# A second attention run in double slots: the scores of two head pairs back to back, with the other steps packed between them

## The reference, cut to what matters

```python
xn = _layernorm(x, ln_gamma, ln_beta)
q = (xn @ w_q).reshape(B, SQ, NUM_HEADS, DIM_HEAD)        # 16 batches, 256 x 16 x 64
k, v = jnp.split(context @ w_kv, 2, axis=-1)
scores = jnp.einsum('bqhd,bkhd->bhqk', q * SCALE, k)
attn = jax.nn.softmax(scores, axis=-1)
out = jnp.einsum('bhqk,bkhd->bqhd', attn, v).reshape(B, SQ, INNER)
out = out @ w_out + b_out
return out * jnp.tanh(gate[0])                            # added to x
```

## Time and profile before

| what | value |
|---|---|
| median of three runs | 1820.49 us (1820.12 to 1822.55) |
| the profiled execution, its span | 1823.8 us |
| PE busy | 1709.7 us, 94% |
| DVE, ACT, POOL busy | 1313.3, 1144.5, 825.5 us (72%, 63%, 45%) |
| second attention, first to last scores | 1039.5 to 1621.8 us |
| scores of pair 16 to scores of pair 126 | 1116.9 to 1618.2 us |

### The profile page before, as it was taken

One profiled execution on the slowest core, in us unless ns is written; L12 is line 12 of the kernel. 1 busy time (PEld: TensorE's weight loads), 2 busy tenths in 40 slices (PEclk: granted clock), 3 DMA queues, 4 the chain that ended last, 5 costly groups with the idle time before them and its releaser, 6 DMA issues.

```text
span 1823.8 us, 41775 instructions
## 1 busy us (share of the span) xinstructions
PE 1709.7 (94%) x16112; PEld 1461.9 (80%) x16112; DVE 1313.3 (72%) x2808; ACT 1144.5 (63%) x2880; POOL 825.5 (45%) x1300
## 2 busy tenths in 40 slices
PE   5799999999999999999999889999999999997778
PEld 4567676679899999999999767888888888876655
DVE  4789989551707888888888486777777777668447
ACT  1377677523347777777777477777777777764330
POOL 2235433110103333333331487888888887764200
PEclk7799999999999999999999999999999999999789
DMA  7755556246876666666676722222222222111378
GB/s 187 207 134 121 128 132 120 80 155 237 295 257 211 243 244 243 243 243 243 244 241 221 243 76 65 93 65 70 63 95 66 69 63 89 53 56 48 99 209 296
DMA packets 131815, 284.99 MB, mean 156 GB/s; under 512 B 13921, under 2 KB 74593, under 8 KB 118945
## 3 DMA queue, kind: packets, MB, share of 16 engines
q1 hardware_dynamic: 110880, 169.81, 30.9%
q0 software_dynamic: 20736, 112.51, 18.1%
HBM read 199.95 MB, written 82.05 MB: 155 GB/s over the span
## 4 chain that ended last, share of the span: by engine, by line
PE 75%; DVE 10%; DMA 5%; POOL 5%; issue 4%; ACT 0%; SPq 0%; DVEq 0%; POOLq 0%; ACTq 0%
PE ps L1250 12%; PE ps L1236 12%; PE ps L1998 5%; PE ps L373 5%; PE ps L219 5%; PE ps L2029 4%; PE ps L1984 4%; PE ps L2018 4%; PE ps L379 4%; PE ps L464 3%; PE ps L440 3%; DVE NM L592 2%; POOL P L209 2%; PE ps L540 2%; PE ps L452 2%
## 5 line engine op out<-in xcount | busy, mean ns | idle before, releaser
L196 ACT ACTIVATE P<-ps,NM 128x256 f32<-128x256 f32 x512 | 236.3, 481 | 127.5 <-DVE NM L185 127.5
L209 POOL TENSOR_TENSOR P<-P,RS 128x1024 f32<-128x1024 f32 x128 | 242.9, 1903 | 73.9 <-DVE RS L203 73.5
L1236 PE MATMUL ps<-XRP,W1P 128*128 128x256 f32 x1872 | 227.1, 281 | 3.3 <-DVE W1P L1319 3.3
L1236 PEld LDWEIGHTS ps<-XRP,W1P 128*128 128x128 f32 x1872 | 220.4, 190 | 3.6 <-DVE W1P L1319 3.6
L1250 PE MATMUL ps<-W2P,HP 128*128 128x256 f32 x1872 | 221.9, 277 | 0.0
L1250 PEld LDWEIGHTS ps<-W2P,HP 128*128 128x128 f32 x1872 | 218.5, 188 | 0.0
L592 DVE TENSOR_REDUCE NM<-ps 128x2 f32<-128x512 f32 x256 | 164.4, 684 | 38.2 <-PE ps L440 36.5
L690 ACT ACTIVATE PT<-ps 128x512 f32<-128x512 f32 x256 | 139.2, 597 | 69.7 <-PE ps L452 67.5
L185 DVE TENSOR_REDUCE NM<-ps 128x2 f32<-128x512 f32 x256 | 164.6, 685 | 5.8 <-PE ps L1984 4.2
L1170 POOL DMA_INDIRECT WE<-in_we,WIX x39 | 44.3, 1135 | 269.2 <-DVE W1P L1319 208.8
L1279 ACT ACTIVATE HF<-ps,WE 128x256 f32<-128x256 f32 x312 | 129.0, 465 | 43.3 <-PE ps L1236 43.3
(11 more groups left out here) (236 smaller groups left out, 3740.2 us busy)
## 6 DMA issues: line engine op xcount, KB each, us to landing
KS<-k_scratch SPq DMA_DIRECT2D x64, 256.0 KB, 2.9
V<-v_scratch SPq DMA_DIRECT2D x16, 1024.0 KB, 6.1
k_scratch<-KVM SPq DMA_DIRECT2D x52, 256.0 KB, 3.9
QS<-q_scratch SPq DMA_DIRECT2D x96, 128.0 KB, 4.4
v_scratch<-KVM SPq DMA_DIRECT2D x40, 256.0 KB, 3.0
ys_scratch<-YS SPq DMA_DIRECT2D x39, 256.0 KB, 8.0
ctx_scratch<-CHL SPq DMA_DIRECT2D x32, 256.0 KB, 2.7
CHR<-ctx_scratch SPq DMA_DIRECT2D x16, 512.0 KB, 4.8
```

The source lines that it names most:

```text
L196: i = e.activation(self.P[u % 4][:, c, :], PS[SB[n % 3]][:, y * 256:y * 256 + 256], ACT.Exp, bias=self.NM[:, u % 4, c:c + 1], accum_out=se ...
L209: e.tensor_tensor(p, p, self.RS[:, u % 4, :].unsqueeze(2).to_broadcast([128, 4, 256]), ALU.mult).then_inc(self.s_pn, 1)
L1236: m = e.matmul(PS[p][:, hh * 256:hh * 256 + 256], W1P[i % 2][wi][:, cc * 1024 + hc * 128:cc * 1024 + hc * 128 + 128], XRP[i % 2][xi][:, cc ...
```

## The change

The same instructions are put in another order, and the banks are dealt out anew. The loop now runs over 64 double slots (`SLOTS1`) and 21 more (`TAIL1`) for the last layer. In double slot i:

- PE: scores of pairs 2i and 2i+1; one half of a result (`results_in`); turn of 2i-2; one part of queries, of index i+2 (`queries_in`); in the first two of a batch's four slots the turn of the next input; turn of 2i-1; values of 2i-3 and 2i-2; from slot 65 the steps of the last layer.
- DVE: split of 2i-5, max of 2i, split of 2i-4, max of 2i+1, result add, reciprocal of 2i, the batch's work, reciprocal of 2i+1, low half of the queries.
- ACT: exp 2i, copies of turn 2i-2, exp 2i+1, copies of turn 2i-1, high half of the queries, keys, norms.
- POOL: norms of 2i and 2i+1, keys, input, newton, fetches.

Banks: 0 to 3 scores, 4 and 5 turns, 6 (`WB`) queries and results together, 7 (`OB1`) values of even pairs in one half, values of odd pairs and the turned input in the other. Since queries and results share a bank, queries wait for the result add of their own slot, and a result waits for the low half of the queries of the slot before. A result is no longer accumulated over eight pairs: each half goes into the bank alone and is added to x by itself, so there are 64 additions instead of 32. Both splits of a slot wait for the values of both pairs (`done`).

Cut to its core:

```diff
     SB, TB, OB = (0, 1, 2), (3, 4), 5
+    SB1, TB1, OB1, WB = (0, 1, 2, 3), (4, 5), PS[7], PS[6]
...
-    QB, RB = PS[7], PS[6]
+    def results_in(i):
+        if i < 5:
+            return ()
+        if i <= SLOTS1:
+            return (i - 5,)
+        return {SLOTS1 + 1: (60, 61), SLOTS1 + 2: (62, 63)}.get(i, ())
+    def queries_in(i):
+        return tuple(d for d in ((1, 2) if i == 0 else (i + 2,)) if d < SLOTS1)
+    def values_in(i):
+        return tuple(u for u in (2 * i - 3, 2 * i - 2) if 0 <= u < U)
+    def results_before(i):
+        return sum(len(results_in(x)) for x in range(i))
...
-            w.wait_ge(a1.s_ex, 2 * u - 1)
+            w.wait_ge(a1.s_ex, 2 * (u - 1))
...
-        def queries(b, n):
+        def queries(d, added):
+            b, n = d // 4, d % 4
             w.wait_ge(s_wl, 2)
             w.wait_ge(s_xs, 2 * b + 2)
-            w.wait_ge(s_qb, 4 * b + n)
+            w.wait_ge(s_qb, d)
+            w.wait_ge(s_rb, added)
...
-        def result(b, lt, half):
+        def result(x, added, asked):
+            b, lt, half, M = result_part(x)
...
-            w.wait_ge(s_rb, 2 * b + lt)
+            w.wait_ge(s_rb, added)
+            w.wait_ge(s_qb, asked)
...
+        for i in range(SLOTS1 + TAIL1):
+            g, n = i // 4, i % 4
+            split = min(max(0, 2 * i - 3), U)
+            for u in (2 * i, 2 * i + 1):
+                if u < U:
+                    scores(u)
+            if i == 0:
+                queries(1, 0)
+            for x in results_in(i):
+                result(x, results_before(i), min(queries_before(i), 64))
+            if 0 <= 2 * i - 2 < U:
+                a1.turn_pe(e, w, 2 * i - 2)
+            for d in queries_in(i)[-1:]:
+                queries(d, results_before(i + 1))
+            if n < 2 and is_batch(g + 1):
+                turn_x(g + 1, n, split)
                 turned += 1
...
+            if 0 <= 2 * i - 1 < U:
+                a1.turn_pe(e, w, 2 * i - 1)
+            for u in values_in(i):
+                values(u, split, turned)
...
+        def values_split(u, done):
             hi, lo = (z[:, u % 8, :] for z in OT1[u // 8 % 2])
...
+            w.wait_ge(a1.s_pv, done)
...
+        for i in range(SLOTS1 + TAIL1):
+            g, n = i // 4, i % 4
+            done = min(max(0, 2 * i - 3), U)
...
+            if 0 <= 2 * i - 5 < U:
+                values_split(2 * i - 5, done)
+            if i < SLOTS1:
+                a1.max_dve(e, w, 2 * i)
+            if 0 <= 2 * i - 4 < U and i <= SLOTS1 + 1:
+                values_split(2 * i - 4, done)
+            if i < SLOTS1:
+                a1.max_dve(e, w, 2 * i + 1)
...
+            for x in results_in(i):
+                result_add(x, results_before(i + 1))
+            if i < SLOTS1:
+                a1.recip_dve(e, w, 2 * i)
+            if n < 2 and is_batch(g + 1):
+                scale_x(g + 1, n)
+            if n < 2 and is_batch(g + 2):
+                add(g + 2, 2 * n)
+                add(g + 2, 2 * n + 1)
+            if n == 1 and is_batch(g - 2) and g < 17:
+                stats_out(g - 2)
+            elif n == 2 and is_batch(g + 2):
                 stats_x(g + 2)
...
+            if i < SLOTS1:
+                a1.recip_dve(e, w, 2 * i + 1)
+            for d in queries_in(i)[-1:]:
+                queries_low(d)
```

More of the change, by code:

```diff
@@ L1988, in scores, with values @@
                             m.then_inc(a1.s_sc, 1)
-        def values(u, turned):
+        def values(u, split, turned):
             b, p = u // 8, u % 8
+            c0, c1 = value_half(u)
             w.wait_ge(d_vl[b % 2], 16 * (b // 2 + 1))
             w.wait_ge(a1.s_tv, 2 * u + 2)
-            w.wait_ge(a1.s_ot, 2 * u)
+            w.wait_ge(a1.s_ot, 2 * split)
             w.wait_ge(s_xh, turned)
@@ L2025, in result @@
             w.wait_ge(a1.s_ot, 2 * (8 * b + 4 * half + 4))
-            w.wait_ge(s_rb, 2 * b + lt)
+            w.wait_ge(s_rb, added)
+            w.wait_ge(s_qb, asked)
             for cc in range(4 * half, 4 * half + 4):
-                for x, (oi, wi) in enumerate(PAIRS):
-                    e.matmul(RB[:, 0:256], OT1[b % 2][oi][:, cc, lt * 128:lt * 128 + 128], W1O[wi][:, cc, :],
-                             start=(cc == 0 and x == 0), stop=False)
+                for n, (oi, wi) in enumerate(PAIRS):
+                    m = e.matmul(M, OT1[b % 2][oi][:, cc, lt * 128:lt * 128 + 128], W1O[wi][:, cc, :],
+                                 start=(cc == 4 * half and n == 0), stop=(not half and cc == 3 and n == 2))
             if half:
                 for j in range(2):
-                    m = e.matmul(RB[:, 0:256], EYE[:, :], BOS[j][:, :], start=False, stop=(j == 1))
-                m.then_inc(s_om, 1)
+                    m = e.matmul(M, EYE[:, :], BOS[j][:, :], start=False, stop=(j == 1))
+            m.then_inc(s_om, 1)
         w.wait_ge(s_ye, NTF)
@@ L2040, in pe_l1 @@
             late_tile(e, w, t)
+        w.wait_ge(s_kve, 125)
         queries(0, 0)
@@ L2043, in pe_l1 @@
         turned = 2
[L2044 to L2073, removed]
-                turned += 1
-            if 0 <= i - 4 < U:
-                values(i - 4, now)
-            if i >= STEP0:
-                pe_step(e, w, i - STEP0)
+        for i in range(SLOTS1 + TAIL1):
[14 more added lines that the diff above has]
+                turn_x(g + 1, n, split)
+                turned += 1
+            if 0 <= 2 * i - 1 < U:
+                a1.turn_pe(e, w, 2 * i - 1)
+            for u in values_in(i):
+                values(u, split, turned)
+            if i > SLOTS1:
+                pe_step(e, w, i - SLOTS1 - 1)
         pe_tail(e, w)
@@ new lines, in dve_l1 @@
+            if 0 <= 2 * i - 5 < U:
[6 more added lines that the diff above has]
+                a1.max_dve(e, w, 2 * i + 1)
+            if i == 0:
+                norms(1, 0)
+                norms(1, 1)
+                queries_low(1)
+            for x in results_in(i):
+                result_add(x, results_before(i + 1))
@@ L2217, in keys_high, with queries_high @@
-        def keys_high(b, n):
-            c = 4 * b + n
+        def queries_high(d):
+            n = d % 4
+            w.wait_ge(s_qm1, d + 1)
+            w.wait_ge(a1.s_sc, scores_read(d))
+            e.activation(flat(Q1[0][:, 2 * n:2 * n + 2, :]), WB[:, :], ACT.Copy).then_inc(s_qh, 1)
+        def keys_high(c):
+            n = c % 4
             w.wait_ge(d_kl_wf1[c % 2], 16 * (c // 2 + 1))
-            w.wait_ge(a1.s_sc, scores_read(b, n))
+            w.wait_ge(a1.s_sc, scores_read(c))
```

253 lines of the change are left out of this document (111 added, 142 removed).

## The result

The changed kernel takes 1852.15 us (median of four runs, 1850.13 to 1860.55) against 1820.3 us before (median of four runs too): 1.0179 times as long, 95% interval 1.0154 to 1.0205. The forecast was 1850.5 us.

A forecast was written before the change was run, and what follows sets the result against it. PE bound the old kernel; in the changed one a ring through PE, ACT and DVE would, 9.12 us a double slot. 527.1 + 4.4 - 501.3 = +30.2 us gives 1850.5 us; own range 1834 to 1868, 8 in 10 range 1822 to 1876.

The forecast's parts named there:

- The ring: Queries to result add to next queries, round PE, ACT and DVE: 9.12 us a double slot without batch work.
- the tie: Before DVE's first split, the ways through PE's values (4.50 us) and ACT's copies (4.48) end together; shortening one gains nothing.
- The wait before queries: PE waits for the result add, 0.5 to 0.8 us in most slots, 1.8 in a batch's second.
- the norm is late: POOL's first norm of a batch's fourth slot comes 0.9 us late, half hidden: +0.4 in 11 batches, 4.4 us.
- PE's own saving: PE's steps per double slot sum to 8.36 us, 8.59 with bias and turned input, against 9.11 before.
- Batch work: Extra on DVE and PE: +0.49 us in a batch's first slot, +1.53 in the second, +0 in third and fourth.
- The sum: Pair 16 to 126, with start and end at 0: 527.1 + 4.4 - 501.3 = +30.2 us.
- Start: The first 16 pairs, 77 us before, keep their time: 0, ends -6 and +8 us.
- End: After the attention, one result half fewer but two turns and values later: 0, ends -4 and +4 us.
- PE as the bound: Rival: DVE's part is 0.5 to 0.8 us shorter, so PE sets the slot; 25 us less, 1795; chance 0.12.
- The clock: Rival: PE's granted clock falls in second slots of a batch, 26 us more, 1877; chance 0.16 together with POOL.
- POOL as the main bound: Rival: POOL later by a further 2.5 us a batch, 27 us more, 1878; chance 0.16 together with the clock.

The follow-up runs named there:

- extra_ring: Changed kernel plus one unused 512-column reduction on DVE in each slot from the ninth, ahead of the result add: 1877.02 us, 1.0334 of the kernel before.
- extra_idle: Changed kernel plus the same unused 512-column DVE reduction, but behind the reciprocal of the first pair: 1845.89 us, 1.0171 of the kernel before.
- high_early: Changed kernel with ACT's high half of the queries before its copies of the second turn: 1847.68 us, 1.0162 of the kernel before.
- add_early: Changed kernel with DVE's result add between the second split and the last two reductions: 1836.84 us, 1.0109 of the kernel before.
- three_moves: Changed kernel with early result add, statistics in the fourth slot and ACT's high half before its copies: 1795.84 us, 0.9874 of the kernel before.
- after_again: The changed kernel run again with no edit, beside the others on one chip: 1846.94 us, 1.0153 of the kernel before.
- add_stats: Changed kernel with the result add ahead of the last reductions and statistics in the fourth slot, ACT's order kept: 1796.57 us, 0.9882 of the kernel before.
- stats_late: Changed kernel with a finished batch's statistics and POOL's newton in the fourth slot, not the second: 1837.79 us, 1.0102 of the kernel before.

## Why the prediction was right, step by step

*The ring.* Right, in place and size. Forecast 9.12 us for a slot without batch work, measured 9.02 to 9.05. Each link has its row above: low half, split, reductions, add without a gap, queries 0.05 after the add. extra_ring and extra_idle show that the ring and not DVE's load is the bound, high_early shows the tie, add_early opens it. The wait before queries (the time from the turn's start, less 0.84) is 0.5, 0.9 and 1.6 us in the batch above and nothing where the norm is late; 0.5 to 0.8 and 1.8 were forecast.

*PE's own saving.* Forecast 8.36 us for a slot's steps, measured 8.25 in the one slot of three_moves where nothing is added to them; with the bias 8.60 and 8.50 to 8.57. Turn before queries was taken as 0.88 and is 0.84.

*Batch work.* First slot: forecast 9.61, measured 9.73; second 10.65 and 10.41; third 9.12 and 9.02. A batch: 38.9 (with 0.4 for POOL) and 38.98. The fourth slot is 9.82 for 9.52: the turn of 1324.91 could have started at 1323.68, 0.23 behind the bias's row as in three_moves, and comes 1.2 us late; the forecast said 0.9, with half of it hidden.

```profile
1322.95 3.75 POOL L210 TENSOR_TENSOR P<-P,RS 128x1024 f32<-128x1024 f32 x2
1327.90 1.89 POOL L210 TENSOR_TENSOR P<-P,RS 128x1024 f32<-128x1024 f32 x1
```

POOL waits for nobody here; its first norm of 1322.95 ends at 1324.86, and the turn follows. The mechanism was right, the size 0.3 us short in each batch.

That a batch meets its forecast to 0.1 us is luck in part: the four errors, +0.12, -0.24, -0.10 and +0.30, cancel. In the first slot the way wasn't the forecast one either. Values start 2.99 us after the queries (1325.76, 1328.75), as reckoned, but the first split comes at 5.30 (1331.06) and not at 4.99: DVE is held up by two expert additions that take 1.87 us for 0.87, a term that the prediction lacks (last section). From there to the queries it is 4.43 us for the 4.62 forecast. Two first slots have no slow addition (queries at 1130.99 and 1598.47); they took 9.56 us, so the slow ones cost 0.17 each.

*The sum.* Forecast 531.5 us (527.1 + 4.4) from pair 16 to pair 126, measured 530.2. Start: 0 with ends -6 and +8, measured +4.7, and +5.0 in the second profile, so this term was too small. End: 0 with ends -4 and +4, measured -3.4, though this part varies: 191.9 us in the second profile. These two nearly cancel. The forecast of +30.2 meets +31.9 in the medians, and +28.9 in those of after_again.

*Rivals.* PE as the bound did not come; it came once the ring was cut (three_moves, 1796 for the 1795 of that rival, though 2.4 us of that are the lower base). Its "for" was DVE's modest load, and that is the thing to distrust. The clock stayed at 1.00 in this stretch of the changed kernel, where PE's longest wait was 1.6 us; it did fall in two of the edited kernels, after waits of 1.9 to 2.4 us, so this rival was nearer than it looks. POOL as the main bound did not come in the changed kernel, but it is what stood next in line in add_early.

What the change lost, then: its saving on PE, 0.27 us a slot for the scores alone, was there all along and was hidden by two orders that came with it: the add behind all reductions, in a bank shared with the queries, and the statistics in the slot where DVE had no room. Changing these two (add_stats) turns +1.5% into -1.2%, and every other part of the change stays, the shared bank too. No run moved the low half or the splits.

## What to carry to other kernels

When steps are packed to save one engine's changes of kind, follow one buffer round all engines, with the durations of each queue's instructions ahead of it, and compare that length with the saving; an engine that is busy for 70% can still be the bound at one place of its order. Where two ways into a step end together, a cut on one shows nothing, and says nothing against the theory. When an experiment lengthens a wait on TensorE, look at the granted clock of its slots before the time is put down to the ring. And a short instruction that frees a shared bank goes ahead of the long ones that free nothing.

## What the runs showed of the hardware

An addition on DVE with two inputs from SBUF (L2119, 128x256) stood still while POOL ran its multiplication of two SBUF inputs. In the changed kernel 13 of the 54 such additions that start after 1060 us began within a POOL norm; 12 of them took 1.45 to 1.48 us and one 1.86, each ending 0.28 to 0.29 us after the norm did, where the other 41 took 0.47 or 0.48. The row at 1328.61 above is one of them with the next behind it: 1.87 us for two, while the norm of 1327.90 runs until 1329.79; the pair at 1338.36 took 0.87. DVE's instructions on PSUM in the same time (reductions, splits) are not slowed. The Trainium skill (SBUF — State Buffer, "SBUF: two separate sides") says that VectorE and GpSimd share a pair of ports as an exclusive lock, held for the whole instruction, and names VectorE instructions with two SBUF inputs among those that take it; the trace agrees. I had counted these additions at 0.39 us each wherever they stood. In the changed kernel the delay fell where it cost 0.17 us; in stats_late a norm met one in eleven first slots, and it took 2.1 us. That the missing 8 us of stats_late are this is read from the rows and wasn't tried alone.

Two inputs aren't the only case. The small TENSOR_SCALAR of 128x2 with one input from SBUF (L131, L133) takes 0.17 us in most places. In stats_late 16 of them began within a norm; they took 1.04 to 1.60 us, and each ended 0.04 us or less after the norm did. The statistics' other instructions (L118, L126) and the reciprocals kept their times inside norms.

Between the scores of pair 16 and those of pair 126 the granted clock fell to 1.2 GHz only behind waits of PE of 1.9 to 2.4 us: behind 3 of the 11 such waits of add_early and 4 of the 11 of extra_ring. No other kernel here has a fall in that stretch; their longest waits are 1.7 us. A slot with a fall in it took 1.2 to 1.6 us more.
